# Routing steps of the second mixer placed differently among the attention heads

## What is computed

```
x = x + L0_attn(layernorm(x))      # gated delta rule
x = x + L0_ffn(layernorm(x))       # 8 experts, 2 per token, and a shared one
x = x + L1_attn(layernorm(x))      # causal attention, 16 heads of 128, 2 kv heads
x = x + L1_ffn(layernorm(x))       # 16 experts, 6 per token
```

```
logits = 30 * tanh(einsum(xq, xk) * SCALE / 30);  masked causally
out    = einsum(softmax(logits), xv) @ Wo
scores = softmax(h @ gate_w.T);  topk_w, topk_idx = top_k(scores, 6)
y      = sum over experts e of cw[:, e] * expert_e(h)
```

## Time and profile before

| | us |
|---|---|
| median of 3 runs | 845.69 (845.59 to 847.47) |
| the profiled execution, its own time | 841.79 |
| its span, first to last instruction | 840.0 |
| TensorE busy in it | 786.3 (94%) |
| VectorE busy | 482.3 (57%) |
| ScalarE busy | 361.3 (43%) |
| GpSimd busy | 218.0 (26%) |

### The profile page before, as it was taken

How to read it: one execution, slowest core, us unless ns; L and a number is a source line. 1 busy time by engine, 2 the same in 40 slices (tenths; PEclk the granted TensorE clock), 3 DMA queues, 4 the chain that set the end, 5 groups by cost and what they waited for, 6 DMA issues and landing times.

```text
span 840.0 us, 14393 instructions
## 1 busy us (share of the span) xinstructions
PE 786.3 (94%) x4825; PEld 544.4 (65%) x4825; DVE 482.3 (57%) x1166; ACT 361.3 (43%) x756; POOL 218.0 (26%) x318
## 2 busy tenths in 40 slices
PE   5988799879989998899999999989999999999998
PEld 3576566666657785677777767766764545455557
DVE  5999866766522225866565565767755463324443
ACT  3988767646123333352332342323246676211111
POOL 3644654111610034111111111116712233200000
PEclk9998999999999999999999999999999999999999
DMA  4001780092343322034442322212333433294431
GB/s 144 2 1 31 231 292 2 2 229 79 107 144 102 101 69 68 21 104 121 144 131 68 101 68 68 76 39 92 113 82 114 134 95 116 73 289 127 126 126 50
DMA packets 95807, 85.72 MB, mean 102 GB/s; under 512 B 34792, under 2 KB 84456, under 8 KB 95736
## 3 DMA queue, kind: packets, MB, share of 16 engines
q1 hardware_dynamic: 88200, 70.05, 28.7%
q0 software_dynamic: 4224, 11.74, 4.1%
q10 hardware_dynamic: 3312, 3.02, 1.1%
HBM read 57.02 MB, written 26.71 MB: 100 GB/s over the span
## 4 chain that ended last, share of the span: by engine, by line
PE 75%; DVE 10%; ACT 7%; issue 4%; DMA 1%; POOL 1%; SPq 0%; ACTq 0%; another core or an unknown queue 0%; DVEq 0%; POOLq 0%
PE bank L1488 9%; PE bank L1451 7%; PE bank L1306 6%; PE bank L1345 6%; PE bank L1267 6%; PE bank L1283 6%; PE bank L1331 5%; PE bank L730 4%; PE bank L756 3%; PE bank L953 3%; PE bank L2309 3%; PE bank L975 2%; ACT arena L2366 2%; PE bank L2266 2%; PE bank L2293 2%
## 5 line engine op out<-in xcount | busy, mean ns | idle before, releaser
L1607 ACT ACTIVATE arena<-bank 128x512 f32<-128x512 f32 (+1 forms) x96 | 46.9, 525 | 147.4 <-PE bank L1451 135.2
L1229 POOL TENSOR_TENSOR arena<-arena,causal_t 128x256 f32<-128x256 f32 x64 | 45.2, 726 | 215.9 <-ACT arena L1612 215.9
L1488 PEld LDWEIGHTS bank<-arena 128*128 128x128 f32 x640 | 76.1, 191 | 4.8 <-POOL arena L1229 3.5
L1488 PE MATMUL bank<-arena 128*128 128x129 f32 x640 | 77.2, 275 | 1.9 <-POOL arena L1229 1.9
L1451 PE MATMUL bank<-arena 128*128 128x512 f32 (+3 forms) x256 | 74.6, 434 | 1.4 <-DVE arena L1685 1.4
L1540 ACT ACTIVATE arena<-bank 128x512 f32<-128x512 f32 (+1 forms) x39 | 20.2, 520 | 123.3 <-PE bank L1267 106.9
L1306 PE MATMUL bank<-arena 128*128 128x256 f32 (+1 forms) x272 | 66.2, 382 | 4.4 <-DVE arena L1665 2.7
L1267 PE MATMUL bank<-xnT,arena 128*128 128x512 f32 (+1 forms) x168 | 65.9, 514 | 0.0
L1306 PEld LDWEIGHTS bank<-arena 128*128 128x128 f32 (+1 forms) x272 | 50.9, 190 | 22.6 <-issue 13.2
L1345 PE MATMUL bank<-arena 128*128 128x256 f32 x256 | 61.0, 381 | 2.5 <-DVE arena L1692 2.0
L1345 PEld LDWEIGHTS bank<-arena 128*128 128x128 f32 x256 | 48.1, 190 | 23.3 <-issue 12.0
(11 more groups left out here) (296 smaller groups left out, 1486.7 us busy)
## 6 DMA issues: line engine op xcount, KB each, us to landing
arena<-in_w_gu SPq DMA_DIRECT2D x44, 256.0 KB, 3.3
rows_in<-place SPq DMA_DIRECT2D x5, 1664.0 KB, 14.4
arena<-in_w_dn SPq DMA_DIRECT2D x34, 128.0 KB, 3.5
rows<-arena SPq DMA_DIRECT2D x8, 544.0 KB, 4.3
arena<-in_w_dn SPq DMA_DIRECT2D x24, 176.0 KB
arena<-in_wq SPq DMA_DIRECT2D x32, 128.0 KB
arena<-in_wo SPq DMA_DIRECT2D x32, 128.0 KB
arena<-rows SPq DMA_DIRECT2D x32, 128.0 KB, 2.1
```

The source lines that it names most:

```text
L1229: nc.gpsimd.tensor_tensor(blocks, blocks, causal_t[:].unsqueeze(1).to_broadcast([P, 2, P]), ALU.mult).then_inc(s_p, 1)
L1488: mm = nc.tensor.matmul(b_o[pair][:, t * (DH + 1):(t + 1) * (DH + 1)], pr[:, o:o + P], v[:, grp, kt, :], start=(kt == 0), stop=(kt == qb))
L1607: nc.scalar.activation(th[:, sbank * 512:sbank * 512 + w], b_s[sbank][:, 0:w], ACT.Tanh, scale=SCALE / SOFTCAP).then_inc(s_th, 1)
```

## The change

Head 18: the transposes `ln_turn(8)` stood ahead of the scores of head 18 and now stand behind them, ahead of the turn. Their copy to `xnT` goes from ScalarE (`ln_evac(8)`) to VectorE (a new `ln_copy`), ahead of `turned(17)`.

Routing of VectorE: `route_b1(2)`, which was soft, over and even behind head 21, is split: soft and over behind head 20, even in head 21 between the copies of the turned outputs and the rotation. `route_b2(2)` (ties and rank) goes from behind head 22 to behind head 21. `route_b3(2)` is split into `route_count` (in head 22, between the copies and the rotation) and `route_mask` (behind head 22).

Places: `places1(0)` on TensorE goes from ahead of the scores of head 24 to behind the scores of head 23, and its read-out `rows1_read` from head 24 to head 23. `rows1_index` goes from behind head 24 to behind head 23 without its last part, which is the new `rows1_place` (the six picks, a reduction, a cast) and stays behind head 24. The sends still begin at head 25.

```diff
+        def ln_copy(self, dve, e):
+            dve.wait_ge(ln_tp, 4 + e + 1)
+            nc.vector.tensor_copy(xnT[:, :, LN[e][0] * P:(LN[e][0] + 2) * P],
+                                  LN_BANK[e][:].rearrange("p (k t) -> p k t", k=KD)).then_inc(ln_xT, 1)
...
         def route_b3(self, dve, r):
+            self.route_count(dve, r)
+            self.route_mask(dve, r)
+
+        def route_count(self, dve, r):
+            self.step(dve, nc.vector.tensor_reduce(scr[r].lg[:], scr[r].gt[:], AX.X, ALU.add))
+
+        def route_mask(self, dve, r):
...
-            step(dve, nc.vector.tensor_reduce(c.lg[:], c.gt[:], AX.X, ALU.add))
...
+        def rows1_place(self, dve, h):
+            c, step = scr[2 + h], self.step
             self.pick(dve, c, c.pos)
...
-                if n == 18:
-                    self.ln_turn(pe, 8)
...
-                if n == 24:
-                    self.places1(pe, 0)
                 pe.wait_ge(s_qr, rot[f"q{n}"] + 1)
...
                     mm.then_inc(s_sc, 1)
+                if n == 18:
+                    self.ln_turn(pe, 8)
+                if n == 23:
+                    self.places1(pe, 0)
                 if n:
                     self.turn(pe, n - 1)
...
-                if n == 24:
+                if n == 23:
                     pe.wait_ge(s_pl, RD1[0])
...
-                if n == 18:
-                    self.ln_evac(act, 8)
...
+                if n == 18:
+                    self.ln_copy(dve, 8)
-                if n == 24:
+                if n == 23:
                     self.rows1_read(dve, 0)
                 if n:
                     self.turned(dve, n - 1)
+                if n == 21:
+                    self.route_even(dve, 2)
+                if n == 22:
+                    self.route_count(dve, 2)
...
+                if n == 20:
+                    self.route_soft(dve, 2)
+                    self.route_over(dve, 2)
                 if n == 21:
-                    self.route_b1(dve, 2)
+                    self.route_b2(dve, 2)
                 if n == 22:
-                    self.route_b2(dve, 2)
+                    self.route_mask(dve, 2)
                 if n == 23:
-                    self.route_b3(dve, 2)
+                    self.rows1_index(dve, 0)
                 if n == 24:
-                    self.rows1_index(dve, 0)
+                    self.rows1_place(dve, 0)
```

## The result

The changed kernel takes 836.99 us (median of 4, 836.49 to 837.50) against 845.98 for the kernel before: ratio 0.9892, interval 0.9875 to 0.9909. Yet in the trace nearly everything is as worked out. The profiled execution has a span of 834.7 us (forecast 833.8) and its own time is 836.49, where that of the kernel before was 841.79: there the difference is 5.3.

What follows compares the result with a forecast made beforehand. TensorE's list plus its holes was taken to bound the kernel. Savings of 1.72 + 0.43 + 2.52 + 0.08 + 1.42 = 6.17 us took the timed median from 845.69 to 839.5, range 837.9 to 842.4.

Steps and rivals of the forecast that it cites:

- heads 17 and 18: Transposes of step 8 moved behind head 18's scores: 17.98 us instead of 19.70 from scores 17 to 19.
- head 22: Spreading three comparisons in a row removes a 0.58 us stall; less 0.15 of costs, heads 20 to 22 save 0.4.
- head 23: Scores 23 to 24: earlier mask ends TensorE's 2.46 us wait; 12.01 becomes 9.49, 2.5 saved.
- the next two: Heads 24 and 25: 8.36 becomes 8.28, 0.1 saved; the split index brings 9.70 down, 1.4 saved.
- wait for the copy out of bank 2: Head 19's queries newly wait for VectorE's copy of the transposes: 0.5 us booked, ends 0.3 and 0.8.
- wait for the read-out: Head 24's queries newly wait for the places' read-out: 0.1 us booked, ends 0 and 0.3.
- late rotation: Count in head 22 makes VectorE's rotation 0.7 late of 0.91 us slack: 0.05 booked, ends 0 and 0.2.
- The part about `route_even`: Head 21: even and GpSimd's mask multiplication both read two SBUF tensors and do not run side by side: 0.1 us booked.
- the prediction's two readings: Who is held up in head 21: the later one, GpSimd, costing 0.1 us, or VectorE's even, making the rotation 0.7 late.
- rival A: VectorE's late work in heads 21 and 22 costs more than booked: saving 4.3 to 5.4, 840.3 to 841.4 us; 24%.
- Rival B: Time saved in the heads is given back later, in the pair loop: up to all 6 lost, 843 to 845.7 us; 7%.
- rival C: GpSimd's sends get longer and delay heads 26 to 29 by 8.8 us: slower, 848.3 us; 3%.

Runs made afterwards that it cites:

- three filling matmuls: Kernel before plus three matmuls that nobody reads, in TensorE's wait for the mask at head 24: 841.31 us against 844.66, ratio 0.9961.
- five filling matmuls: Kernel before plus five matmuls that nobody reads, in TensorE's wait for the mask at head 24: 844.32 us against 845.90, ratio 0.9975.
- two counts: Changed kernel with the count step ahead of the rotation of head 22 done twice: 839.65 us, ratio 0.9919.
- routing spread: Kernel before with only VectorE's routing steps spread, places and index left where they were: 838.47 us, ratio 0.9928.
- wait of 2.97: Changed kernel with the count step done three more times behind head 22's divisions, so TensorE waits for the mask: 844.16 us, ratio 0.9965.

## Why the prediction was wrong

**The terms in the heads were right.** By the distances between scores, heads 17 and 18 saved 1.65 (forecast 1.72), head 22 saved 0.58 (0.43, with head 21, which stayed at 8.28), head 23 saved 2.55 (2.52), and the next two 0.1 and 1.4 as forecast. The wait for the copy out of bank 2 was 0.35 and the copy took 0.69, the value taken from the rotation step; booked were 0.5. The wait for the read-out was 0, where 0.1 was booked. The late rotation cost nothing: it ended at 541.96, 0.26 before the scores. The part about `route_even` (L585 here) and the mask multiplication was right in kind:

```profile
529.05 1.22 DVE L585 TENSOR_TENSOR arena<-arena 128x1024 f32<-128x1024 f32 x1
529.84 1.70 POOL L1243 TENSOR_TENSOR arena<-arena,causal_t 128x256 f32<-128x256 f32 x2 [6.88 <-ACT arena L1624]
531.02 0.69 DVE L1694 TENSOR_TENSOR arena<-bank,arena 64x512 f32<-64x512 f32 x1
```

GpSimd's pair took 1.70 in place of 1.41 and ended at 531.54, before the values at 531.70. The rotation step of the third row, which reads one of its inputs from PSUM, ran beside GpSimd and was not held up. Even took 1.22, what such a comparison takes alone (1.23 in the earlier trace rows): of the prediction's two readings, that even pays or that the one which comes second does, this row bears out the second. The greatest length in the changed kernel's mask line above, 1012 ns against 733 before, is this pair. That rules out rival A. (Its price was also slightly off its own terms: 6.17 less 1.75 leaves 4.4, and the upper ends of the waits alone leave 5.7, where 4.3 to 5.4 stands.) Rival B, that the time is given back later, fell by 219.2 and 219.1 behind the loop, and rival C, that the sends get in the way, by the scores of heads 25 to 30, which follow each other at 8.27 or 8.28.

**The step that failed** is "The timed median lies 3.9 above the profiled execution for reasons that the profile doesn't show; I take the same difference off it." The 3.9 was not a constant beside the kernel. Between the two traces of the kernel before the difference is 4.1, and 3.0 of it lies in the loop, in the very stretch that the change edits: 3.2 in head 24 (the first table's 23), behind the wait that the change removes, less 0.2 in other heads. The other 1.1 lies ahead of the loop, and the profiled execution of the changed kernel has it too. (It is no fixed amount either: in a second trace of the changed kernel the loop begins at 342.4.) So the 2.46 us wait was priced at 2.46 where it cost 2.46 + 3.2 in the one ordinary execution of this kernel that was traced. With that term the sum is 6.2 + 3.2 = 9.4 against 9.0 measured. The forecast of the profiled execution, 835.6, was 0.9 off its 836.49, for the 1.1 ahead of the loop.

What could have been seen beforehand: the profiled execution was faster than all timed ones, by more than their spread (845.59 to 847.47), and the clock behind its waits was 1.00 in the whole loop and behind the 2.48 us at 246. A case "the ordinary execution loses its clock behind the 2.46 us wait" was missing among the rivals. It could not be priced from a row behind that wait; but the 3.9 itself was a bound for it, and the range's lower end should have gone to it.

Open are: what decides in which execution the clock falls (1.66 kept it, 1.46 lost it), and how often the wait of head 24 costs how much, since three traces show it and the rest are times; and the rest of the spread of single executions, up to 850.6 for the kernel before, part of which showed as further half-clock stretches near 110 us in one trace (three filling matmuls), near 330 in two (five filling matmuls, two counts) and near 190 and 655 in one each (routing spread, wait of 2.97).

## What to carry to other kernels

When the profiled execution is faster than the timed ones by more than their spread, the difference has a place; look for it (granted clock by stretch, a second profile of the same kernel) before you subtract it as a constant. In this kernel a wait of TensorE of one and a half to three us ahead of the counts cost its length and, in four of five traces, 1.6 to 3.2 us more in clock, so such a wait is the first to remove; and where what it waits for couldn't come earlier, matmuls that nobody reads, of no more than its length, gave back the second half. Free places on another engine can be read off the distance between what it ended and who waits for it; here the place of 0.91 ahead of the scores took a rotation 0.65 later at no cost, and a further count step of 1.24 came out almost whole, at 1.17, on the critical path.

## What the runs showed of the hardware

- TensorE fell to its lower level behind waits of 2.46 us (in two of three traces that have this wait), 2.97 and even 1.46 us, each in a stretch that was otherwise dense; the loss was 3.2 and 1.6, 3.1 and 2.0 us. It did not fall behind 2.46 and 2.48 us in the first trace of the kernel before, nor behind the 1.66 us of head 18 in either trace. Three filling matmuls, 2.1 us long, kept the clock at 1.00.
- An instruction of VectorE with two SBUF inputs and one of GpSimd held each other up: 1.38 for 0.43 on VectorE, 1.70 for 1.41 on GpSimd. A VectorE reduction over one SBUF input in head 22 of the changed kernel, beside the same GpSimd work, did not: 1.21, as alone, and GpSimd's pair 1.41.
- A float32 matmul of 384 columns shows as two in the trace and took 0.65 us (five of them from 556.88 to the next matmul at 560.11).
